# First rows' root mostly on VectorE, keys split ahead of the weights, and GpSimd scaling the output projection's pieces itself

## The chip, the cores and the metric

The kernel runs on one core of one Trainium2 chip. The metric is device time in microseconds (us) for one execution. The kernel before took 2051.89 us (median of three runs, 2051.29 to 2052.78).

## The reference

Sixteen sequences of 256 rows with 512 columns go through one layer. First a layer norm, then cross attention with 16 heads of 128 on a context of the same size, added to the input; then a second layer norm and a gated feed-forward part with block-quantised operands, added again. The first half is what the change touches:

```python
x = x + _L0_xattn_ref(_layernorm(x), ctx, Wq, Wk, Wv, Wo)
    q = (inputs_q @ Wq).reshape(b, sq, H, HD) * (1.0 / np.sqrt(HD))
    k = (inputs_kv @ Wk).reshape(b, skv, H, HD)
    v = (inputs_kv @ Wv).reshape(b, skv, H, HD)
    attn = softmax(einsum('bqhd,bkhd->bhqk', q, k))
    return einsum('bhqk,bkhd->bqhd', attn, v).reshape(b, sq, H * HD) @ Wo
x = x + _L0_ffn_ref(_layernorm(x), w_gate, w_up, w_down)
```

## The kernel before

All five engines run one program each, with an order written out by hand and counting semaphores between them. The attention part goes over 64 quads of four steps each; a step i = 4n + k is one head group. In a step TensorE does, in this order, the key projection K and the query projection (12 matmuls each into one bank), the context product of an earlier step, the scores, the value projection V (12), and from step 5 on the output projection (6) (`quad` in the TensorE program). To keep accuracy each float32 operand is split into two float16 parts: an upper part that ScalarE writes (`hi`, L610) and a lower part, the operand times its scale less the upper part, that VectorE writes (`lo`, L762). K of step i+1 waits for VectorE's lower part of q and k of step i.

The attention weights come in four chunks of eight pieces of 1024 columns. Pieces 0, 2, 4, 6 hold query and key weights, 1 and 5 value weights (`V_AT`), 3 and 7 output weights (`O_AT`). Each is staged in float32 and split the same way: ScalarE's upper part (L618), then VectorE's lower part for even pieces. For odd pieces ScalarE also writes the staged piece back multiplied by its scale (L621), and GpSimd subtracts (L442). Pieces 0 to 3 of chunk 0 (`EARLY` = 4) are split ahead of the first quad, the other 28 two per step, an even and an odd one, in the first 14 steps: in steps 0, 2, 4, ... the odd one is of the value weights, in steps 1, 3, 5, ... of the output weights. GpSimd waits for `piece_hi`, and TensorE waits for the lower parts by `wait_split`. SyncE's queue reloads a staging place when its piece has been subtracted.

Ahead of the first quad, VectorE takes the statistics of the first 256 rows (L977, L980), GpSimd computes the reciprocal root with a power and one Newton step in six small operations (`rstd`, L433 to L438), VectorE normalises (L777), and TensorE transposes through the identity (L1191), behind 30 warm-up matmuls on zeroed data (L1187). The split of the first keys and of xT follows.

In a step VectorE's order is: lower part of q and k, maximum (L923), lower part of the context, on some steps one operation of a later x or key row, scaling of the row sums (L940), their reciprocal (L943), lower part of v, lower part of the probabilities (L950), and last its piece of the weights. ScalarE's is: upper part of q and k, of the context, the even piece, the exponentials (L654), upper part of v, of the probabilities (L664), on some steps one of a key or x row, and the odd piece.

Of the kernel before, what the change touches and what calls it, by code (L numbers as in the profile page):

```python
# [36 lines left out]
ALU = mybir.AluOpType  # L37
# [3 lines left out]
P = 128  # L41
# [23 lines left out]
EARLY = PIECES - QUAD  # L65


QK_AT, V_AT, O_AT = (0, 2, 4, 6), (1, 5), (3, 7)
# [13 lines left out]
def build(nc, kvt, wattn, wffn, xtok, out):  # L82
# [4 lines left out]
    with ctx:  # L87
# [60 lines left out]
        def free_part(chunk, part, pc, pieces):  # L148
# [27 lines left out]


        names = """waited ident_ready zeroed first_x_loaded first_kv_loaded
            first_stats first_aggr first_step first_rstd first_xn first_tr first_hi first_kv_hi first_lo
            stage_loaded0 stage_loaded1 stage_loaded2 stage_loaded3 piece_hi piece_lo_even piece_lo_odd  # L180
            x_loaded kv_loaded stats_done aggr_done rstd_step rstd_done xn_ready x_hi x_lo xT_loaded kv_hi kv_lo
            s_done max_done exp_done sum_scaled rec_done
            qk_done qk_hi qk_lo c_done c_hi c_lo v_done v_hi v_lo p_hi p_lo pt_loaded0 pt_loaded1 o_done o_added
# [12 lines left out]
        def wait_apart(eng, name, value):  # L196

            eng.wait_ge(sm[name], value)
            eng.sem_inc(sm["waited"], 1)  # L199
# [17 lines left out]
        def piece(chunk, pc, part):  # L217
            return wall[:, bass.ds(chunk * (2 * WCHUNK) + part * WCHUNK + pc * PIECE, PIECE)]
# [5 lines left out]
        def staged(chunk, pc):  # L224

            if isinstance(chunk, int) and chunk == 0:
                return first_stage[:, pc * PIECE:(pc + 1) * PIECE]
            return stages[pc % SLOTS]
# [172 lines left out]
        def _(eng):  # L401
# [22 lines left out]
            def rstd(rows, width, aggr, step, done, m):  # L424

                def then(ins, k):
                    ins.then_inc(sm[step], 1)
                    wait_apart(eng, step, 5 * m + k)
                wait_apart(eng, aggr, m + 1)
                r = [rs[0:rows, width * a:width * (a + 1)] for a in range(6)]  # L430
                var = mv[0:rows, 1:2 * width:2]
                half_, eps = [powers[0:rows, a:a + 1].to_broadcast([rows, width]) for a in range(2)]
                then(eng.tensor_tensor(r[1], var, eps, ALU.add), 1)  # L433
                then(eng.tensor_tensor(r[2], r[1], half_, ALU.pow), 2)
                then(eng.tensor_tensor(r[3], r[2], r[2], ALU.mult), 3)
                then(eng.tensor_tensor(r[4], r[3], r[1], ALU.mult), 4)
                then(eng.tensor_scalar(r[5], r[4], -0.5, 1.5, ALU.mult, ALU.add), 5)
                eng.tensor_tensor(r[0], r[2], r[5], ALU.mult).then_inc(sm[done], 1)  # L438

            def split_piece(chunk, pc):  # L440
                wait_apart(eng, "piece_hi", chunk * PIECES + pc + 1)
                eng.tensor_tensor(piece(chunk, pc, 1), staged(chunk, pc), piece(chunk, pc, 0), ALU.subtract  # L442
                                  ).then_inc(sm["piece_lo_odd"], 1)

# [90 lines left out]

            load_x(0)
            load_kv(0)
            rstd(P, 2, "first_aggr", "first_step", "first_rstd", 0)
            slot1 = acc[:, 2 * D:4 * D].rearrange("p (t d) -> p t d", t=2)
            eng.dma_start(slot1, xtok[0].rearrange("t p d -> p t d")).then_inc(sm["acc_loaded"], 16)  # L540
            for pc in range(1, EARLY, 2):
# [65 lines left out]
        def _(eng):  # L607
# [4 lines left out]
            def split_piece(chunk, pc):  # L612
                if isinstance(chunk, int) and chunk == 0:
                    eng.wait_ge(sm["first_loaded"][pc], 16)
                else:
                    eng.wait_ge(sm[f"stage_loaded{pc % SLOTS}"],
                                16 * ((chunk - 1) * (PIECES // SLOTS) + pc // SLOTS + 1))
                last = eng.activation(piece(chunk, pc, 0), staged(chunk, pc), ACT.Copy, scale=W_SCALE)  # L618
                if pc % 2:

                    last = eng.activation(staged(chunk, pc), staged(chunk, pc), ACT.Copy, scale=W_SCALE)  # L621
                last.then_inc(sm["piece_hi"], 1)
# [66 lines left out]


            eng.preload_act_table(ACT.Exp)
            split_piece(0, 0)
            for m in range(QPB):
                hi(prep_slot(kvT, m, 0), first_kv(m), X_SCALE, "first_kv_loaded", 16, "first_kv_hi")
            split_piece(0, 1)
            for tile_ in range(2):
                hi(first_slot(xT, tile_, 0), first_bank[tile_][:, :].rearrange("p (c f) -> p c f", c=KC), X_SCALE,
                   "first_tr", tile_ + 1, "first_hi")
            for pc in range(2, EARLY):
                split_piece(0, pc)  # L700
            def even(n):
                return None if n % 2 else n // 2
# [54 lines left out]
        def _(eng):  # L757
# [214 lines left out]

            eng.wait_ge(sm["first_x_loaded"], 16)
            for tile_ in range(2):
                eng.bn_stats(stat[:, 6 * tile_:6 * tile_ + 6], half(first_x, tile_)).then_inc(sm["first_stats"], 1)  # L977
# [1 line left out]
            for tile_ in range(2):  # L979
                last = eng.bn_aggr(mv[:, 2 * tile_:2 * tile_ + 2], stat[:, 6 * tile_:6 * tile_ + 6])  # L980
            last.then_inc(sm["first_aggr"], 1)
            split_piece(0, 0)
            eng.wait_ge(sm["first_rstd"], 1)
            for tile_ in range(2):
                apply(half(first_norm, tile_), half(first_x, tile_), P, tile_).then_inc(sm["first_xn"], 1)
            for m in range(QPB):
                lo(prep_slot(kvT, m, 1), first_kv(m), prep_slot(kvT, m, 0), X_SCALE,
                   "first_kv_hi", m + 1, "first_lo")
            for tile_ in range(2):
                lo(first_slot(xT, tile_, 1), first_bank[tile_][:, :].rearrange("p (c f) -> p c f", c=KC),  # L990
                   first_slot(xT, tile_, 0), X_SCALE, "first_hi", tile_ + 1, "first_lo")
# [313 lines left out]
```

## Time and profile before

| | |
|---|---|
| median of three runs | 2051.89 us |
| profiled execution | 2051.55 us |
| its span, first to last instruction | 2050.0 us |
| TensorE busy | 2021.3 us, 99% |
| VectorE busy | 1536.7 us, 75% |
| ScalarE busy | 1000.2 us, 49% |
| GpSimd busy | 740.2 us, 36% |

In a timeline row the first number is the start in us from the start of the span, the second the time from the start of the group to the end of its last operation; in brackets stands how long the engine sat idle before it and what ended that. PE is TensorE, DVE VectorE, ACT ScalarE, POOL GpSimd, SP SyncE. Operations of one engine are pipelined, so the end of one lies up to 0.1 us (on TensorE 0.16) behind the start of the next.

### The profile page before, as it was taken

The page shows a single profiled execution, that of the slowest core. Times are in us where ns is not written, and L with a number is a line of the kernel's source. Part 1 is how long each engine was busy: PE and PEld are TensorE (multiplying, and loading weights), DVE is VectorE, ACT ScalarE, POOL GpSimd, SP SyncE. Part 2 cuts the span into 40 slices and gives each one's busy share as a digit, 9 for nine tenths or more (in the row PEclk, how much of TensorE's full clock was granted, in tenths as well). Part 3 has the DMA queues.
Part 4 walks back from the last instruction along what each step waited for, and adds up shares of the span by engine and source line. Part 5 has one row for each costly group of instructions (what it writes and reads, how often), then busy time and mean ns, then how long its engine had stood idle before and what let it go on. Part 6 is the DMA issues. An engine that isn't in the chain of part 4 may idle for free. (4 is left out here: it accounts for less than half of the span.)

```text
span 2050.0 us, 45754 instructions
## 1 busy us (share of the span) xinstructions
PE 2021.3 (99%) x15430; PEld 1506.2 (73%) x15430; DVE 1536.7 (75%) x3340; ACT 1000.2 (49%) x2682; POOL 740.2 (36%) x881
## 2 busy tenths in 40 slices
PE   8999999999999999999999999999999999999998
PEld 6888878788888888878888888888888874444443
DVE  6767777777777877777777777776665558888887
ACT  8955545455555455555454555455555453222332
POOL 5422232323333333323333333331111006777776
PEclk9999999999999999999999999999999999999999
DMA  8834444444444444444444445443333274454554
GB/s 257 211 72 84 86 91 86 91 90 86 90 91 91 91 88 87 91 91 91 91 86 87 90 89 91 91 86 72 69 70 71 55 168 80 78 92 83 88 87 85
DMA packets 455038, 193.26 MB, mean 94 GB/s; under 512 B 418400, under 2 KB 431200, under 8 KB 454848
## 3 DMA queue, kind: packets, MB, share of 16 engines
q1 hardware_dynamic: 432640, 139.52, 35.3%
q0 software_dynamic: 15872, 44.97, 9.2%
q10 hardware_dynamic: 6336, 6.29, 1.0%
q8 instruction: 112, 1.84, 0.4%
q14 instruction: 78, 0.64, 0.1%
HBM read 61.21 MB, written 27.26 MB: 43 GB/s over the span
## 5 line engine op out<-in xcount | busy, mean ns | idle before, releaser
L1097 PE MATMUL b_qk<-kvT,attn_weights 128*128 128x256 f16 x3072 | 377.2, 273 | 3.5 <-DVE qk L762 2.9
L1097 PE MATMUL b_v<-attn_weights,kvT 128*128 128x256 f16 x3072 | 377.2, 273 | 0.0
L1097 PE MATMUL b_qk<-xT,attn_weights 128*128 128x256 f16 x3072 | 377.2, 273 | 0.0
L654 ACT ACTIVATE prob<-b_s,nmax 128x256 f32<-128x256 f32 x514 | 239.2, 470 | 276.1 <-DVE nmax L923 274.2
L1097 PEld LDWEIGHTS b_qk<-kvT,attn_weights 128*128 128x128 f16 x3072 | 300.2, 98 | 92.7 <-issue 4.9
L950 DVE SCALAR_TENSOR_TENSOR psplit<-prob,rrec,psplit 128x256 f16<-128x256 f32 x514 | 306.5, 637 | 79.2 <-ACT psplit L664 79.2
L762 DVE SCALAR_TENSOR_TENSOR qk<-b_qk,qk 128x512 f16<-128x512 f32 x256 | 176.7, 690 | 246.0 <-ACT qk L610 238.4
L610 ACT ACTIVATE qk<-b_qk 128x512 f16<-128x512 f32 x256 | 152.5, 596 | 426.4 <-PE b_qk L1097 426.2
L1097 PEld LDWEIGHTS b_qk<-xT,attn_weights 128*128 128x128 f16 x3072 | 300.6, 98 | 34.8
L1097 PEld LDWEIGHTS b_v<-attn_weights,kvT 128*128 128x128 f16 x3072 | 300.6, 98 | 34.8
L664 ACT ACTIVATE psplit<-prob,rrec 128x256 f16<-128x256 f32 x514 | 233.0, 500 | 67.8 <-DVE rrec L943 67.8
L1097 PE MATMUL b_c<-probT,vbuf 128*128 128x256 f16 x1554 | 212.0, 273 | 3.1 <-DMA probT<-psplit 3.0
L1097 PE MATMUL b_s<-qk 128*128 128x256 f16 x1542 | 210.3, 273 | 0.0
L1152 PE MATMUL b_o<-attn_weights,cbuf 128*128 128x512 f16 x768 | 186.6, 379 | 0.0
L1152 PE MATMUL b_w<-attn_weights,cbuf 128*128 128x512 f16 x768 | 186.6, 379 | 0.0
L923 DVE TENSOR_REDUCE nmax<-b_s 128x2 f32<-128x512 f32 x257 | 177.1, 689 | 3.7 <-PE b_s L1097 3.3
L1097 PEld LDWEIGHTS b_c<-probT,vbuf 128*128 128x128 f16 x1554 | 151.3, 98 | 23.2 <-DMA probT<-psplit 4.5
L1097 PEld LDWEIGHTS b_s<-qk 128*128 128x128 f16 x1542 | 150.9, 98 | 17.4
L463 POOL TENSOR_TENSOR ffn_magic_rounded<-ffn_y,ffn_magic_rounded 128x512 f32<-128x512 f32 x48 | 60.7, 1265 | 230.1 <-DVE ffn_magic_rounded L823 230.1
L566 POOL TENSOR_TENSOR attn_weights<-attn_weights,inner_scale 128x1024 bf16<-128x1024 bf16 x63 | 120.2, 1908 | 49.2 <-DVE attn_weights L1028 43.1
L421 POOL DMA_DIRECT2D kvrow<-kvt x61 | 35.6, 584 | 241.9 <-DVE kvT L762 218.7
L1152 PEld LDWEIGHTS b_w<-attn_weights,cbuf 128*128 128x128 f16 x768 | 75.1, 98 | 63.8
(133 smaller groups left out, 2642.0 us busy)
## 6 DMA issues: line engine op xcount, KB each, us to landing
ffn_w<-wffn SPq DMA_DIRECT2D x48, 256.0 KB, 2.9
acc<-xtok POOLq DMA_DIRECT2D x16, 512.0 KB, 4.9
out<-acc POOLq DMA_DIRECT2D x16, 512.0 KB, 3.3
xrow<-xtok POOLq DMA_DIRECT2D x31, 256.0 KB, 3.2
kvrow<-kvt POOLq DMA_DIRECT2D x61, 128.0 KB, 2.4
out<-attn_weights POOLq DMA_DIRECT2D x30, 256.0 KB, 4.5
stage<-wattn SPq DMA_DIRECT2D x12, 512.0 KB, 4.6
ffn_scratch<-ffn_t SPq DMA_DIRECT2D x48, 128.0 KB, 2.5
```

The source lines that it names most:

```text
L421: eng.dma_start(kvrow[:, :], kvt[bass.ds((r + QPB) & (NQ - 1), 1), :, :].rearrange("g p f -> p (g f)")).then_inc(sm["kv_loaded"], 16)
L463: eng.tensor_tensor(wr, wy[:, :], wc, ALU.add).then_inc(sm["ffn_add"], 1)
L566: eng.tensor_tensor(by_block(q), by_block(q), spread(i_scale), ALU.mult).then_inc(sm["i_q"], 1)
L610: eng.activation(dst, src, ACT.Copy, scale=scale).then_inc(sm[done], 1)
L654: last = eng.activation(half(prob, q, 256), half(bS, q, 256), ACT.Exp, bias=nmax[:, q:q + 1], scale=1.0, accum_out=rsum[:, q:q + 1])
L664: eng.activation(p_part(k, q, 0), half(prob, q, 256), ACT.Copy, scale=rrec[:, q:q + 1]).then_inc(sm["p_hi"], 1)
L762: eng.scalar_tensor_tensor(out=dst, in0=src, scalar=scale, in1=hi_part, op0=ALU.mult, op1=ALU.subtract).then_inc(sm[done], 1)
L923: eng.tensor_reduce(nmax[:, :], bS[:, :].rearrange("p (q f) -> p q f", q=2), AX_X, ALU.max, negate=True).then_inc(sm["max_done"], 1)
L950: last = eng.scalar_tensor_tensor(out=p_part(k, z, 1), in0=half(prob, z, 256), scalar=rrec[:, z:z + 1], in1=p_part(k, z, 0), op0=ALU.mult, ...
L1097: last = eng.matmul(out, l, r, start=(a == 0), stop=(a == len(pairs) - 1))
L1152: last = eng.matmul(o_bank[tile_][:, :], l, r, start=(u % 8 == 0 and at == 0), stop=(u % 8 == 7 and at == len(pairs) - 1))
```

## The change

Three things. The reciprocal root of the first rows: the sum with epsilon and the Newton step go to VectorE (`first_rstd`), and GpSimd keeps the power alone. The order ahead of the first quad: ScalarE splits the first keys ahead of piece 0, and piece 1 after the two xT operations; VectorE subtracts piece 0 after the keys. The odd pieces of the output weights (3 and 7): ScalarE writes only the upper part, and GpSimd multiplies the staged piece by the scale, waits for itself (`piece_scaled`) and then subtracts.

```diff
@@ -439,6 +439,11 @@
 
             def split_piece(chunk, pc):
                 wait_apart(eng, "piece_hi", chunk * PIECES + pc + 1)
+                if pc in O_AT:
+                    at = chunk * len(O_AT) + O_AT.index(pc) + 1
+                    eng.tensor_scalar(staged(chunk, pc), staged(chunk, pc), W_SCALE, None, ALU.mult
+                                      ).then_inc(sm["piece_scaled"], 1)
+                    wait_apart(eng, "piece_scaled", at)
                 eng.tensor_tensor(piece(chunk, pc, 1), staged(chunk, pc), piece(chunk, pc, 0), ALU.subtract
                                   ).then_inc(sm["piece_lo_odd"], 1)
 
@@ -535,7 +540,9 @@
 
             load_x(0)
             load_kv(0)
-            rstd(P, 2, "first_aggr", "first_step", "first_rstd", 0)
+            wait_apart(eng, "first_step", 1)
+            eng.tensor_tensor(rs[:, 4:6], rs[:, 2:4], powers[:, 0:1].to_broadcast([P, 2]), ALU.pow
+                              ).then_inc(sm["first_pow"], 1)
             slot1 = acc[:, 2 * D:4 * D].rearrange("p (t d) -> p t d", t=2)
             eng.dma_start(slot1, xtok[0].rearrange("t p d -> p t d")).then_inc(sm["acc_loaded"], 16)
             for pc in range(1, EARLY, 2):
@@ -616,7 +623,7 @@
                     eng.wait_ge(sm[f"stage_loaded{pc % SLOTS}"],
                                 16 * ((chunk - 1) * (PIECES // SLOTS) + pc // SLOTS + 1))
                 last = eng.activation(piece(chunk, pc, 0), staged(chunk, pc), ACT.Copy, scale=W_SCALE)
-                if pc % 2:
+                if pc in V_AT:
 
                     last = eng.activation(staged(chunk, pc), staged(chunk, pc), ACT.Copy, scale=W_SCALE)
                 last.then_inc(sm["piece_hi"], 1)
@@ -689,14 +696,13 @@
 
 
             eng.preload_act_table(ACT.Exp)
-            split_piece(0, 0)
             for m in range(QPB):
                 hi(prep_slot(kvT, m, 0), first_kv(m), X_SCALE, "first_kv_loaded", 16, "first_kv_hi")
-            split_piece(0, 1)
+            split_piece(0, 0)
             for tile_ in range(2):
                 hi(first_slot(xT, tile_, 0), first_bank[tile_][:, :].rearrange("p (c f) -> p c f", c=KC), X_SCALE,
                    "first_tr", tile_ + 1, "first_hi")
-            for pc in range(2, EARLY):
+            for pc in range(1, EARLY):
                 split_piece(0, pc)
             def even(n):
                 return None if n % 2 else n // 2
@@ -972,6 +978,22 @@
 
 
 
+            def first_rstd():
+
+                def then(ins, k):
+                    ins.then_inc(sm["first_step"], 1)
+                    eng.wait_ge(sm["first_step"], k)
+                eng.wait_ge(sm["first_aggr"], 1)
+                r = [rs[:, 2 * a:2 * a + 2] for a in range(6)]
+                eps = powers[:, 1:2].to_broadcast([P, 2])
+                eng.tensor_tensor(r[1], mv[:, 1:4:2], eps, ALU.add).then_inc(sm["first_step"], 1)
+                eng.wait_ge(sm["first_pow"], 1)
+                then(eng.tensor_tensor(r[3], r[2], r[2], ALU.mult), 2)
+                then(eng.tensor_tensor(r[4], r[3], r[1], ALU.mult), 3)
+                then(eng.tensor_scalar(r[5], r[4], -0.5, 1.5, ALU.mult, ALU.add), 4)
+                eng.tensor_tensor(r[0], r[2], r[5], ALU.mult).then_inc(sm["first_rstd"], 1)
+                eng.wait_ge(sm["first_rstd"], 1)
+
             eng.wait_ge(sm["first_x_loaded"], 16)
             for tile_ in range(2):
                 eng.bn_stats(stat[:, 6 * tile_:6 * tile_ + 6], half(first_x, tile_)).then_inc(sm["first_stats"], 1)
@@ -979,13 +1001,13 @@
             for tile_ in range(2):
                 last = eng.bn_aggr(mv[:, 2 * tile_:2 * tile_ + 2], stat[:, 6 * tile_:6 * tile_ + 6])
             last.then_inc(sm["first_aggr"], 1)
-            split_piece(0, 0)
-            eng.wait_ge(sm["first_rstd"], 1)
+            first_rstd()
             for tile_ in range(2):
                 apply(half(first_norm, tile_), half(first_x, tile_), P, tile_).then_inc(sm["first_xn"], 1)
             for m in range(QPB):
                 lo(prep_slot(kvT, m, 1), first_kv(m), prep_slot(kvT, m, 0), X_SCALE,
                    "first_kv_hi", m + 1, "first_lo")
+            split_piece(0, 0)
             for tile_ in range(2):
                 lo(first_slot(xT, tile_, 1), first_bank[tile_][:, :].rearrange("p (c f) -> p c f", c=KC),
                    first_slot(xT, tile_, 0), X_SCALE, "first_hi", tile_ + 1, "first_lo")
```

ScalarE's program ahead of the first quad, before. `attn_weights<-attn_weights` is a weight piece, `kvT<-attn_weights` a row group of the first keys, `xT<-` the transposed first rows; the last row is the first operation of step 0.

```order
L618 ACTIVATE attn_weights<-attn_weights 128x1024
L610 ACTIVATE kvT<-attn_weights 128x4x64 x4
L618 ACTIVATE attn_weights<-attn_weights 128x1024
L621 ACTIVATE attn_weights<-attn_weights 128x1024
L610 ACTIVATE xT<-b_x 128x4x128
L610 ACTIVATE xT<-b_w 128x4x128
L618 ACTIVATE attn_weights<-attn_weights 128x1024 x2
L621 ACTIVATE attn_weights<-attn_weights 128x1024
L610 ACTIVATE qk<-b_qk 128x512
```

And after:

```order
L617 ACTIVATE kvT<-attn_weights 128x4x64 x4
L625 ACTIVATE attn_weights<-attn_weights 128x1024
L617 ACTIVATE xT<-b_x 128x4x128
L617 ACTIVATE xT<-b_w 128x4x128
L625 ACTIVATE attn_weights<-attn_weights 128x1024
L628 ACTIVATE attn_weights<-attn_weights 128x1024
L625 ACTIVATE attn_weights<-attn_weights 128x1024 x2
L617 ACTIVATE qk<-b_qk 128x512
```

Piece 1, two operations that stood ahead of the two xT rows, stands behind them, and the scaled copy of piece 3 is gone.

GpSimd's program from the first root to the root of the next rows (`128x1`), before:

```order
L433 TENSOR_TENSOR rs<-mv,minus_half_and_eps 128x2
L434 TENSOR_TENSOR rs<-rs,minus_half_and_eps 128x2
L435 TENSOR_TENSOR rs<-rs 128x2
L436 TENSOR_TENSOR rs<-rs 128x2
L437 TENSOR_SCALAR rs<-rs 128x2
L438 TENSOR_TENSOR rs<-rs 128x2
L540 DMA acc<-xtok 128x2x512
L442 TENSOR_TENSOR attn_weights<-attn_weights 128x1024 x2
L433 TENSOR_TENSOR rs<-mv,minus_half_and_eps 128x1
```

And after:

```order
L544 TENSOR_TENSOR rs<-rs,minus_half_and_eps 128x2
L547 DMA acc<-xtok 128x2x512
L447 TENSOR_TENSOR attn_weights<-attn_weights 128x1024
L444 TENSOR_SCALAR attn_weights<-attn_weights 128x1024
L447 TENSOR_TENSOR attn_weights<-attn_weights 128x1024
L433 TENSOR_TENSOR rs<-mv,minus_half_and_eps 128x1
```

One power is left of the six operations, and ahead of the subtraction of piece 3 there is a multiply (L444).

## Rows read from the trace of the kernel before

**Rows 1.** The page, busy time of each engine.
```profile
PE 2021.3 (99%) x15430; PEld 1506.2 (73%) x15430; DVE 1536.7 (75%) x3340; ACT 1000.2 (49%) x2682; POOL 740.2 (36%) x881
```

**Rows 2.** Waits of TensorE, 44 to 1680 us: engine, line waited for: us in total, times, longest.
```profile
PE b_c L1097 <- DMA probT<-psplit: 3.0, 3, 1.1
```

**Rows 3.** Timeline of TensorE at the start: start us, us, operation, [idle before <-releaser].
```profile
5.00 6.36 PE L1187 MATMUL b_s<-vbuf 128*128 128x256 f16 x30 [5.00 <-POOL vbuf L413]
...
11.19 0.60 PE L1191 MATMUL b_x<-ident,attn_weights 128*128 128x128 f32 x4
...
12.82 1.47 PE L1097 MATMUL b_qk<-kvT,attn_weights 128*128 128x256 f16 x12 [0.60 <-DVE kvT L762]
...
18.06 1.47 PE L1097 MATMUL b_qk<-kvT,attn_weights 128*128 128x256 f16 x12
...
23.64 1.47 PE L1097 MATMUL b_qk<-kvT,attn_weights 128*128 128x256 f16 x12 [0.18 <-DVE qk L762]
...
42.57 1.47 PE L1097 MATMUL b_qk<-kvT,attn_weights 128*128 128x256 f16 x12 [1.27 <-DVE qk L762]
...
49.10 1.47 PE L1097 MATMUL b_qk<-kvT,attn_weights 128*128 128x256 f16 x12
```

**Rows 4.** Timeline of ScalarE at the start.
```profile
12.32 0.59 ACT L610 ACTIVATE xT<-b_w 128x512 f16<-128x512 f32 x1
...
15.64 0.60 ACT L610 ACTIVATE qk<-b_qk 128x512 f16<-128x512 f32 x1
...
22.20 0.57 ACT L610 ACTIVATE qk<-b_qk 128x512 f16<-128x512 f32 x1
...
27.35 1.04 ACT L621 ACTIVATE attn_weights<-attn_weights 128x1024 f32<-128x1024 f32 x1
...
28.30 0.58 ACT L610 ACTIVATE qk<-b_qk 128x512 f16<-128x512 f32 x1
...
34.45 0.57 ACT L610 ACTIVATE qk<-b_qk 128x512 f16<-128x512 f32 x1
...
41.13 0.57 ACT L610 ACTIVATE qk<-b_qk 128x512 f16<-128x512 f32 x1
...
47.59 0.57 ACT L610 ACTIVATE qk<-b_qk 128x512 f16<-128x512 f32 x1
```

**Rows 5.** Timeline of VectorE at the start.
```profile
11.26 1.42 DVE L762 SCALAR_TENSOR_TENSOR kvT<-attn_weights,kvT 128x256 f16<-128x256 f32 x4
...
13.89 1.86 DVE L762 SCALAR_TENSOR_TENSOR attn_weights<-attn_weights 128x1024 f16<-128x1024 f32 x1
...
18.82 0.14 DVE L940 TENSOR_SCALAR rsum<-rsum 128x2 f32<-128x2 f32 x1
...
25.18 0.17 DVE L940 TENSOR_SCALAR rsum<-rsum 128x2 f32<-128x2 f32 x1 [0.26 <-ACT prob L654]
...
26.93 1.22 DVE L762 SCALAR_TENSOR_TENSOR attn_weights<-attn_weights 128x1024 f16<-128x1024 f32 x1
...
43.27 0.80 DVE L762 SCALAR_TENSOR_TENSOR xsplit<-xnorm,xsplit 128x512 f16<-128x512 f32 x1
```

**Rows 6.** The weights' tile, 0 to 45 us: duration ns min/median/max, first and last start.
```profile
L762 DVE SCALAR_TENSOR_TENSOR attn_weights<-attn_weights x4: 1218/1222/1859, 8.6 to 26.9; 128x1024 f16<-128x1024 f32 x4
```

**Rows 7.** Timeline of GpSimd at the start.
```profile
11.92 2.75 POOL L442 TENSOR_TENSOR attn_weights<-attn_weights 128x1024 f16<-128x1024 f32 x1 [0.43 <-ACT attn_weights L621]
...
15.93 2.13 POOL L442 TENSOR_TENSOR attn_weights<-attn_weights 128x1024 f16<-128x1024 f32 x1 [1.26 <-ACT attn_weights L621]
```

**Rows 8.** Timeline of VectorE, 271 to 273 us.
```profile
271.82 0.65 DVE L940 TENSOR_SCALAR rsum<-rsum 128x2 f32<-128x2 f32 x1 [0.76 <-ACT prob L654]
```

**Rows 9.** Timeline of GpSimd, 271 to 273 us.
```profile
271.40 1.05 POOL L470 TENSOR_TENSOR ffn_b<-ffn_magic_rounded,ffn_scale 128x512 bf16<-128x512 f32 x1 [3.65 <-DMA ffn_t<-ffn_b]
```

**Rows 10.** GpSimd's clip of 512 columns (L467): duration ns min/median/max.
```profile
L467 POOL TENSOR_SCALAR ffn_magic_rounded<-ffn_magic_rounded x48: 606/614/892, 136.4 to 1369.0; 128x512 f32<-128x512 f32 x48
```

**Rows 11.** DMA issues: count, KB each, median us to landing.
```profile
ffn_magic_rounded<-wattn SPq DMA_DIRECT2D x6, 512.0 KB, 4.9
```

More of the change, by code:

```diff
@@ L178, in build @@
         names = """waited ident_ready zeroed first_x_loaded first_kv_loaded
-            first_stats first_aggr first_step first_rstd first_xn first_tr first_hi first_kv_hi first_lo
-            stage_loaded0 stage_loaded1 stage_loaded2 stage_loaded3 piece_hi piece_lo_even piece_lo_odd
+            first_stats first_aggr first_step first_pow first_rstd first_xn first_tr first_hi first_kv_hi first_lo
+            stage_loaded0 stage_loaded1 stage_loaded2 stage_loaded3 piece_hi piece_scaled piece_lo_even piece_lo_odd
             x_loaded kv_loaded stats_done aggr_done rstd_step rstd_done xn_ready x_hi x_lo xT_loaded kv_hi kv_lo
```

## The prediction

> **What bounds the kernel now.** I read four views, in this order. The page first: TensorE is busy for 99% of the span [rows 1], so a change that leaves its work alone can give back only what TensorE waits. Then the waits of TensorE in the attention part from 44 us on: three waits of about 1 us each for a transposing DMA, and nothing else in 1636 us [rows 2]. So from 44 us to the feed-forward part TensorE sets the pace, and whatever the change does to the other engines there is hidden unless it comes late by more than their slack. The feed-forward part at the end has none of the changed lines. Then the timeline of TensorE at the start, and there the room is. The reader is to look at the starts of the key projections K(i), i counting the steps of one head, four to a quad. One step is 18.06 - 12.82 = 5.24 us of matmuls. From K(1) to K(5) it takes 42.57 - 18.06 = 24.51 us for 4 x 5.24 = 20.96, so 3.55 us are stalls. From step 5 on the output projection joins, a step is 49.10 - 42.57 = 6.53 us, and there are no stalls [rows 3]. Last the timelines of ScalarE, VectorE and GpSimd there. I call A(i) the start of ScalarE's first operation of step i, the upper half of q and k. VectorE's lower half follows it, and K(i+1) starts 1.44 us after A(i): 23.64 after 22.20, 42.57 after 41.13 [rows 3, 4]. A(i) follows A(i-1) by 6.56, 6.10, 6.15, 6.68 and 6.46 us [rows 4]. That is ScalarE's own work, most of it on weight pieces, and it is more than 5.24. So up to K(5) ScalarE is the bound, and from there TensorE is by a hair: A(5) + 1.44 = 49.03, K(6) at 49.10.
>
> The sum is made against the profiled execution, 2051.55 us (span 2050.0 and 1.55 around it), which lies 0.34 under the median of the three runs, 2051.89.
>
> **The root of the first rows.** Six small GpSimd operations become one there and five on VectorE. On paper the root is ready some 1.9 us sooner. But the transposes that need it stand in TensorE's queue behind 30 warm-up matmuls, which start at 5.00, end at 11.36 by the profile and have the first transpose close behind them, at 11.19 [rows 3]. Neither the warm-up nor the clearing of its operand changes. So the transposes don't move, nor does ScalarE's second upper half of xT at 12.32 [rows 4]. Gain: nothing. If this cover were gone it would be up to 1.9 us at the very start.
>
> **Piece order on ScalarE.** The keys' upper halves go ahead of piece 0, which costs nothing, since ScalarE then waits for the transposes anyway. But piece 1 and its scaled copy, two operations that filled that wait, now stand behind the xT operations. Before, three operations of a piece lay between 12.32 + 0.48 = 12.80 and A(0) = 15.64, 0.95 us each [rows 4]. Now there are four (piece 1 twice, piece 2, piece 3): A(0) = 12.80 + 4 x 0.95 = 16.60, 0.95 later.
>
> **Who holds whom.** Three rows of before show that VectorE and GpSimd hold each other. VectorE's subtraction of piece 2 took 1.86 us where its kind takes 1.22; GpSimd's subtraction had 0.78 to go when it started (11.92 + 2.75 = 14.67 against 13.89), so the hold was 0.64 [rows 5 to 7]. GpSimd's took 2.75 instead of 2.13 while VectorE's four key operations ran to 12.68, 0.76 into it [rows 5, 7]. And the tiny scaling of the row sums took 0.65 us instead of 0.17 when GpSimd had 0.63 to go [rows 5, 8, 9]. Each hold is what the other has to go, less 0.15. I use that rule.
>
> In the Trainium skill, GPSIMD Engine Reference, section Key points, the shared SBUF interfaces are said to collide with VectorE instructions that have two SBUF inputs or run in a 2-port mode. Only the second half could cover the row-sum scaling, which has one input of two elements; were it not covered, rival B below would be the case. The trace's 0.65 us speaks for a hold, in one instance.
>
> **The first step.** Piece 1's scaled copy on ScalarE is 13.75 to 14.79; GpSimd's subtraction starts 0.19 after such an end (15.74 to 15.93 [rows 4, 7]), so 14.98 to 17.11. VectorE's subtraction of piece 2 is issued at 15.78 and held 1.18, to 18.18. Behind it queue the lower half of q and k, which could start at 17.2 and starts at 18.1, 0.87 late, then the maximum and the row sums. GpSimd's new multiply of piece 3 is ready when its subtraction ends, but VectorE's waiting operation goes first: held until about 18.0, then 1.03, its subtraction 19.3 to 21.4. The multiply is not in the trace. Nearest is a GpSimd tensor_scalar on 512 columns at 0.61 us [rows 10]; with 0.19 of it fixed, 1024 columns are 1.03. The other end is 2.13, the two-input operation on the same size [rows 7]. I take 1.03, since it is the same kind. The row sums are scaled 3.18 us after A(0) (18.82 after 15.64 [rows 4, 5]), here 0.87 more: 20.65, inside GpSimd's subtraction, with 0.75 to go: held 0.60. So A(1) = 22.20 + 0.95 + 0.87 + 0.60 = 24.62.
>
> **The output projection's pieces.** ScalarE loses one operation, 0.95 us (28.30 - 27.35), for each of pieces 3 and 7 of four chunks [rows 4]. GpSimd gains a multiply, a wait for it and 0.19 us. Let A' be the A that is earlier by 0.95. The multiply is issued at A' + 0.29, held by VectorE's subtraction of the even piece until A' + 0.80 (26.93 + 1.22 = 28.15 against 27.35 [rows 4, 5]), less 0.15, and ends at A' + 1.68. The subtraction then lies at A' + 1.88 to A' + 4.01.  The next row sums are scaled at A' + 2.98 (25.18 - 22.20), with 1.03 to go: held 0.88. The reciprocal, ScalarE's upper half of the probabilities, its pieces and the next A queue behind. So an edit that takes off 0.95 gives back 0.88. In an odd quad (steps 4 to 7) the first step has VectorE's lower half of x at A + 2.14 ahead of the row sums (43.27 - 41.13), and there ScalarE's x operation lets the multiply run unheld: subtraction A' + 1.51 to A' + 3.64, lower half held 1.35, row sums 1.11 late.
>
> The sum, step by step:
> - A(2) = 24.62 + 6.10 - 0.95 = 29.77 (before 28.30)
> - A(3) = 29.77 + 6.15 + 0.88 = 36.80 (34.45)
> - A(4) = 36.80 + 6.68 - 0.95 = 42.53 (41.13)
> - A(5) = 42.53 + 6.46 + 1.11 = 50.10 (47.59)
> - K(6) = 50.10 + 1.44 = 51.54 against 49.10: 2.4 us later.
>
> After that TensorE's 6.53 a step outruns ScalarE's: A(6), after 5.2 in a step without the scaled copy, is 55.3, so K(7) would be 56.7 by it and is 58.07 by TensorE; the lag is no longer added to and never recovered. The pieces come in time: piece 3 of chunk 1 is subtracted at 42.53 + 3.64 = 46.2, its projection is due at 42.53 + 1.44 + 5.24 = 49.2. The next load into its staging place, 4.9 us [rows 11], is there by 51.5, and ScalarE wants it after 54. The forecast is 2051.55 + 2.44 = 2054.0, on the median's footing 2054.3. That is the predicted time, and the rivals below are on the median's footing too.
>
> **Rivals.** B: the row sums are not held, only operations with two large inputs. For it: one instance of the hold in the trace; against it: its size fits the rule. Then 0.60 and 0.88 go and nothing else: A(5) is 48.62, K(6) 50.06, 1.0 later, 2052.9.
>
> C: no new holds at all, GpSimd's longer work slips between VectorE's. A(1) is then 23.15, A(2) 28.30, A(3) 34.45, A(4) 40.18, K(5) 41.62, and K(6) is TensorE's at 48.15: 0.95 sooner, 2050.9. Against it: three holds in the rows.
>
> D: the full gain that the stalls allow, 3.55 plus some 0.3 at K(0), if the transposes did come early: 2048.0. Against it is the warm-up [rows 3].
>
> E: the multiply costs 2.13. Each subtraction moves 1.1 back. The first row sums are held 1.8 instead of 0.6, those of step 2 up to 2.0 instead of 0.88, those of step 4 0.8 more: 3.1 more in all, 2057.4. It decides slower from a multiply of about 1.6 us on, where half of this is reached. Against it: the 0.61 us at 512 columns.
>
> **How the numbers follow.** Forecast A 0.60, B 0.15, C 0.08, D 0.03, E 0.12, and 0.02 for other losses. About 0.2% (4.1 us) is what a measurement of this kernel can tell from no change: below 2047.8 is faster, above 2056.0 slower. A has its own range of 2053.2 to 2056.2, and a little of it lies above, so slower has 0.12 + 0.02 + 0.02 = 0.16. D reaches the limit only just, faster has 0.03. Same has 0.81. The range takes in C and half of E: 2050.8 to 2057.0.
>
> **What would show it.** TensorE's transposes stay at 11.2; A(0) at 16.6; the value projection of step 0 waits for piece 1 and starts near 17.2; VectorE's subtraction of piece 2 lasts 2.4 us; GpSimd's multiplies last about 1.03 alone; row-sum scalings of 0.8 to 1.0 us after pieces 3 and 7; K(6) at 51.5, and 6.53 a step from there. Wrong if the multiply lasts over 1.6 us, if the row sums stay at 0.17 us with GpSimd busy, or if K(6) is at or under 49.1.

## The result

The changed kernel takes 2054.64 us (median of 22 runs, 2052.72 to 2056.54). The kernel before took 2051.61 us beside it on the same chip (22 runs, 2048.89 to 2053.67). The ratio is 1.0015, with a 95% interval of 1.0009 to 1.0021: 3.0 us more. The interval does not hold 1, so the loss is real, but it is smaller than the 0.2% (4.1 us) within which the prediction counts a time as no change. The profiled execution took 2055.55 us, with a span of 2053.5.

### The profile after

The busy line of the page, answering to [rows 1], and TensorE's waits from 44 to 1680 us, answering to [rows 2]:

```profile
PE 2024.2 (99%) x15430; PEld 1510.7 (74%) x15430; DVE 1555.9 (76%) x3345; ACT 999.3 (49%) x2674; POOL 762.6 (37%) x884
```

```profile
PE b_c L1119 <- DMA probT<-psplit: 3.2, 2, 2.2
```

TensorE is busy for 2.9 us more, though its work is the same: a hint that it ran slowly somewhere. GpSimd has 22 us more, although five small operations left it: at least 2.8 for each of the eight multiplies. And one of the waits on the transposing DMA is 2.2 us.

The timeline of TensorE at the start, answering to [rows 3] (start, duration, engine, line, operation, and in brackets the idle time before it and what ended it):

```profile
4.99 4.77 PE L1209 MATMUL b_s<-vbuf 128*128 128x256 f16 x30 [4.99 <-POOL vbuf L413]
9.60 0.60 PE L1213 MATMUL b_x<-ident,attn_weights 128*128 128x128 f32 x4
...
12.14 1.48 PE L1119 MATMUL b_qk<-kvT,attn_weights 128*128 128x256 f16 x12 [1.51 <-DVE attn_weights L768]
...
24.12 1.47 PE L1119 MATMUL b_qk<-kvT,attn_weights 128*128 128x256 f16 x12 [1.32 <-DVE qk L768]
...
49.57 1.47 PE L1119 MATMUL b_qk<-kvT,attn_weights 128*128 128x256 f16 x12
...
54.55 0.83 PE L1119 MATMUL b_c<-probT,vbuf 128*128 128x256 f16 x6 [2.20 <-DMA probT<-psplit]
...
56.18 2.77 PE L1119 MATMUL b_v<-attn_weights,kvT 128*128 128x256 f16 x12
...
60.14 1.47 PE L1119 MATMUL b_qk<-kvT,attn_weights 128*128 128x256 f16 x12
```

The transposes start at 9.60, not 11.19, and the first key projection at 12.14, 0.68 sooner than before. K(6) starts at 49.57, only 0.47 later than before. Then, inside step 6, the context product waits 2.20 us for the transposed probabilities, and the matmuls behind it run slowly. K(7) starts at 60.14. Before it was at 55.64, 6.54 behind 49.10. So K(7) is 4.5 us late, and 4.0 of it came in that one step.

The same timeline of GpSimd, answering to [rows 7]:

```profile
13.40 2.12 POOL L447 TENSOR_TENSOR attn_weights<-attn_weights 128x1024 f16<-128x1024 f32 x1 [4.99 <-ACT attn_weights L628]
15.50 3.74 POOL L444 TENSOR_SCALAR attn_weights<-attn_weights 128x1024 f32<-128x1024 f32 x1
19.43 2.13 POOL L447 TENSOR_TENSOR attn_weights<-attn_weights 128x1024 f16<-128x1024 f32 x1 [0.18 <-POOL attn_weights L444]
...
29.28 3.15 POOL L444 TENSOR_SCALAR attn_weights<-attn_weights 128x1024 f32<-128x1024 f32 x1 [2.65 <-ACT attn_weights L625]
...
41.88 2.77 POOL L444 TENSOR_SCALAR ffn_magic_rounded<-ffn_magic_rounded 128x1024 f32<-128x1024 f32 x1 [3.34 <-ACT attn_weights L625]
44.84 2.13 POOL L447 TENSOR_TENSOR attn_weights<-ffn_magic_rounded,attn_weights 128x1024 f16<-128x1024 f32 x1 [0.18 <-POOL ffn_magic_rounded L444]
46.91 0.79 POOL L538 DMA_DIRECT2D acc<-xtok  x1
47.70 0.56 POOL L417 DMA_DIRECT2D xrow<-xtok  x1
```

The multiply (L444) lasts 2.77 us undisturbed, where the forecast had 1.03. The subtraction of piece 3 of chunk 1 ends at 46.97, and GpSimd issues its two loads behind it. In the kernel before it ended at 43.53:

```profile
41.40 2.13 POOL L442 TENSOR_TENSOR attn_weights<-ffn_magic_rounded,attn_weights 128x1024 f16<-128x1024 f32 x1 [4.54 <-ACT ffn_magic_rounded L621]
```

The end of the subtraction also frees SyncE's reload of the staging place. In SyncE's queue (SPq, the start of the issue), after and then before:

```profile
47.00 0.33 SPq L266 DMA_DIRECT2D ffn_magic_rounded<-wattn  x1
47.81 1.24 SPq L284 DMA_TRANSPOSE probT<-psplit  x1
```

```profile
43.55 0.33 SPq L266 DMA_DIRECT2D ffn_magic_rounded<-wattn  x1
46.16 1.24 SPq L284 DMA_TRANSPOSE probT<-psplit  x1
```

Before, the reload had 2.6 us of lead on the transposing DMA of step 4, and GpSimd's loads stood at 43.5 and 44.2. Now 1.25 MB of loads are issued between 46.91 and 47.70, and the transposing DMA right behind them. The DMA view from 44 to 60 us has (KB each where given, median us from issue to landing), after and then before:

```profile
probT<-psplit SPq DMA_TRANSPOSE x2, 6.8
```

```profile
probT<-psplit SPq DMA_TRANSPOSE x3, 4.0
```

These are medians of the few transposing DMAs in that stretch. The one of step 4, taken alone, landed 6.7 us after its issue in the changed kernel, at 54.51, and 4.0 us after it before. The context product starts at 54.55, so the 2.20 us are this late landing.

The landing is late for two reasons. The DMA was issued 1.65 us later (47.81 against 46.16), since GpSimd held VectorE's lower half of the probabilities just ahead of it (2.06 us instead of 0.88; the rest is the 0.47 of K(6)), and it took 2.7 us longer. Before, it landed at 50.12, 1.6 us ahead of its reader at 51.73, and in the changed kernel the reader was due at 52.35. Worked out from these numbers, the late issue alone would have made no wait (47.81 + 4.0 = 51.8), and the slow transfer alone about 0.5 us (46.16 + 6.7 = 52.9).

The view by stretches (columns: busy us of TensorE, its weight loads, VectorE, ScalarE, GpSimd, then the granted clock) shows the slow matmuls behind the wait: the clock was granted at 0.50, the lower of its two levels, 1.2 GHz.

```profile
54.00:56.00 2.00, 1.45 (x12) 1.23 (x13) 0.70 (x2) 0.38 (x1) 2.00 (x1) 0.89 0.98 365
56.00:58.00 2.00, 2.00 (x11) 1.45 (x10) 1.02 (x2) 0.71 (x1) 1.81 (x2) 0.50 1.52 179
58.00:60.00 2.00, 2.00 (x11) 1.11 (x10) 0.67 (x3) 1.78 (x7) 1.62 (x2) 0.76 1.11 145
```

From the context product to the projection is 54.55 to 60.14, 5.59 us, for what takes 3.91 before (51.73 to 55.64): 1.7 us for the clock. In the kernel before:

```profile
51.73 0.82 PE L1097 MATMUL b_c<-probT,vbuf 128*128 128x256 f16 x6
```

VectorE, answering to [rows 5, 8]:

```profile
8.61 1.00 DVE L783 TENSOR_SCALAR attn_weights<-attn_weights,mv,rs 128x512 f32<-128x512 f32 x2
...
14.19 2.41 DVE L768 SCALAR_TENSOR_TENSOR attn_weights<-attn_weights 128x1024 f16<-128x1024 f32 x1 [0.90 <-ACT attn_weights L625]
...
18.98 0.29 DVE L946 TENSOR_SCALAR rsum<-rsum 128x2 f32<-128x2 f32 x1
...
20.05 2.18 DVE L956 SCALAR_TENSOR_TENSOR psplit<-prob,rrec,psplit 128x256 f16<-128x256 f32 x2 [0.26 <-ACT psplit L671]
...
24.82 2.10 DVE L768 SCALAR_TENSOR_TENSOR kvT<-kvrow,kvT 128x256 f16<-128x256 f32 x1
...
33.29 2.13 DVE L956 SCALAR_TENSOR_TENSOR psplit<-prob,rrec,psplit 128x256 f16<-128x256 f32 x2 [0.32 <-ACT psplit L671]
...
45.59 2.06 DVE L956 SCALAR_TENSOR_TENSOR psplit<-prob,rrec,psplit 128x256 f16<-128x256 f32 x2 [0.31 <-ACT psplit L671]
```

The normalisation starts at 8.61 instead of 10.34. GpSimd's subtractions hold VectorE, but not where forecast: the row sums take 0.29 us, and the two operations on the probabilities behind them take 2.1 to 2.2 instead of 0.88, because the longer multiply moved the subtraction past the row sums. In step 1 the subtraction of a value piece holds the lower half of a key row, 2.10 us instead of 0.58. ScalarE, answering to [rows 4], starts its steps at 14.99, 22.52, 28.99, 35.46, 41.59 and 48.06.

At the end of the attention part the last key projection starts at 1682.00 us, 1.7 later than before (1680.27), not 4.5. In the rest of that part the kernel before has three waits of about 1 us on this DMA [rows 2] and the changed one has one. From there to the end of the span, mostly the feed-forward part, whose lines the change does not touch, it took 371.5 us against 369.7. In this profile the clock stood at 0.50 in two stretches there (1759 to 1762 and 1892 to 1895 us), in that of the kernel before at 1.00 in the same work. A second profile of the changed kernel (`e9_changed_again`, below) has neither stretch and took 369.1, so this difference can't be put down to the change. The slow stretches also add to TensorE's busy time. A single pair of profiles is therefore no measure of 3 us. The medians are.

### The profile page after: what moved, and what is told of

Same layout as the page of the kernel before. It is cut to its first block and busy times, and to the rows that moved or that the text cites. A ratio compares the mean times of both kernels' runs of the same rounds, so it can differ in the third digit from the quotient of the medians.

```text
span 2053.5 us, 45757 instructions
## 1 busy us (share of the span) xinstructions
PE 2024.2 (99%) x15430; PEld 1510.7 (74%) x15430; DVE 1555.9 (76%) x3345; ACT 999.3 (49%) x2674; POOL 762.6 (37%) x884
## 5 line engine op out<-in xcount | busy, mean ns | idle before, releaser
L956 DVE SCALAR_TENSOR_TENSOR psplit<-prob,rrec,psplit 128x256 f16<-128x256 f32 x514 | 316.4, 656 | 80.2 <-ACT psplit L671 80.2
```

The lines of the kernel that those rows point to most:

```text
L956: last = eng.scalar_tensor_tensor(out=p_part(k, z, 1), in0=half(prob, z, 256), scalar=rrec[:, z:z + 1], in1=p_part(k, z, 0), op0=ALU.mult, ...
```

## The experiments

The theory after the result: the time is lost by the long multiply, through the late loads and the transposing DMA. The rivals: the new order ahead of the first quad costs it; or held VectorE operations do, as forecast. The first four kernels tell these apart, e5, e6 and e8 test the mends, and e7, e9 and e10 show how the first microseconds vary. Where a ratio is given, the kernel ran 11 times and the kernel before 27 times; e3, e7, e9 and e10 have one profiled run each.

**Each half alone.** `e1_scale_only` is the kernel before with GpSimd's scaling, `e2_root_and_order` the changed kernel with ScalarE's scaling. The edit of the second, against the changed kernel:

```diff
-                if pc in O_AT:
-                    at = chunk * len(O_AT) + O_AT.index(pc) + 1
-                    eng.tensor_scalar(staged(chunk, pc), staged(chunk, pc), W_SCALE, None, ALU.mult
-                                      ).then_inc(sm["piece_scaled"], 1)
-                    wait_apart(eng, "piece_scaled", at)
...
-                if pc in V_AT:
+                if pc % 2:
```

> The kernel before with the GpSimd scaling of the output weights' pieces alone; root and order are as before. Theory M (the loss comes from GpSimd's multiply, 2.77 us where 1.03 was reckoned, which ends its subtraction late and so delays loads and transposes): all of the loss is here, K(7) 3 to 5 us behind before's 55.64, the time 2 to 4 us above before (ratio 1.001 to 1.002). Theory O (the loss comes from piece 1's place behind the xT operations on ScalarE, the scaling only passes it on): K(6) at 48.2 to 49.5, no wait of over 1 us before step 7, the time within 0.5 us of before.

> The changed kernel with the scaling of the output weights' pieces given back to ScalarE; root and order stay changed. Theory M: the loss is gone, K(0) some 0.7 us earlier than before if the warm-up ends early and A(0) within 0.5 us of it, K(6) between 48.5 and 50.0, the time within 1 us of before (0.9995 to 1.0005). Theory O: K(6) at 50 or later and the time 1 to 3 us above before.

Measured: 2055.35 us with the scaling alone, ratio 1.0017 (1.0008 to 1.0026), and 2052.21 with root and order alone, 1.0003 (0.9994 to 1.0012). The second is 1.1 us above the kernel before, unresolved, where under 1 was expected. The scaling carries the loss. TensorE's timeline with the scaling alone:

```profile
11.15 0.66 PE L1196 MATMUL b_x<-ident,attn_weights 128*128 128x128 f32 x4 [1.16 <-DVE attn_weights L782]
...
49.90 1.47 PE L1102 MATMUL b_qk<-kvT,attn_weights 128*128 128x256 f16 x12
...
54.56 0.83 PE L1102 MATMUL b_c<-probT,vbuf 128*128 128x256 f16 x6 [1.88 <-DMA probT<-psplit]
...
58.48 1.47 PE L1102 MATMUL b_qk<-kvT,attn_weights 128*128 128x256 f16 x12
```

The same wait in the same place, without the half clock behind it: K(7) is 2.8 late, a little under the 3 to 5 expected. The kernel with root and order alone has no wait there (K(6) 49.34, K(7) 55.87).

**What the multiply costs by its form.** `e3_forms` computes the eight multiplies in four forms:

```diff
+                    if form in (0, 4):
+                        eng.tensor_scalar(st, st, W_SCALE, None, ALU.mult).then_inc(sm["piece_scaled"], 1)
+                    if form in (1, 5):
+                        eng.tensor_scalar(st, st, W_SCALE, 1.0, ALU.mult, ALU.mult).then_inc(sm["piece_scaled"], 1)
+                    if form in (2, 6):
+                        eng.tensor_scalar(half(st, 0), half(st, 0), W_SCALE, None, ALU.mult)
...
+                    if form in (3, 7):
+                        eng.tensor_tensor(st, st, powers[:, 2:3].to_broadcast([P, PIECE]), ALU.mult
```

> The changed kernel with the multiply in four forms on the eight pieces, in order: pieces 1 and 5 one operation with one immediate on 1024 columns as in the change, 2 and 6 the same with a second multiply by 1.0, 3 and 7 two operations of 512 columns, 4 and 8 a tensor_tensor with a broadcast constant. If it is the form with one immediate that is slow: 2.77 us for forms one and three (2 x 1.4) and about 1.1 to 1.2 for form two, as the clip of 512 columns with two immediates at 0.61 says. If it is the size: two times 0.6 for form three, 2.7 for one and two. If it is writing back in place: all forms 2.1 or more. The tensor_tensor is expected at 2.1 to 2.7 us, as the subtraction's 2.13.

GpSimd's timeline:

```profile
30.85 1.42 POOL L449 TENSOR_SCALAR attn_weights<-attn_weights 128x1024 f32<-128x1024 f32 x1 [2.64 <-ACT attn_weights L636]
...
43.62 1.50 POOL L451 TENSOR_SCALAR ffn_magic_rounded<-ffn_magic_rounded 128x512 f32<-128x512 f32 x1 [3.62 <-ACT attn_weights L636]
45.10 1.48 POOL L452 TENSOR_SCALAR ffn_magic_rounded<-ffn_magic_rounded 128x512 f32<-128x512 f32 x1
...
55.49 2.27 POOL L455 TENSOR_TENSOR ffn_magic_rounded<-ffn_magic_rounded,minus_half_and_eps 128x1024 f32<-128x1024 f32 x1 [2.78 <-ACT attn_weights L636]
```

With two immediates (L449) 1.42 us, partly held; with one, 1.48 us for each 512 columns; as a two-input operation 2.27. The same element count, type and engine: only the form of the instruction differs. The row that the forecast scaled from [rows 10] is a clip, which has two immediates. This kernel was the slowest, 2060.38 us. Its TensorE shows the same wait and the same slow matmuls:

```profile
57.77 0.83 PE L1130 MATMUL b_c<-probT,vbuf 128*128 128x256 f16 x6 [3.53 <-DMA probT<-psplit]
...
59.42 2.77 PE L1130 MATMUL b_v<-attn_weights,kvT 128*128 128x256 f16 x12
```

**The collision taken apart.** `e4_acc_early` issues the 512 KB load of `acc` ahead of the late subtraction:

```diff
+                        if isinstance(r, int) and r == 0 and k == QUAD - 1:
+                            eng.dma_start(acc[:, 0:2 * D].rearrange("p (t d) -> p t d", t=2),
+                                          xtok[1:2].rearrange("b t p d -> p (b t) d")).then_inc(sm["acc_loaded"], 16)
...
-                    if more and (q == 0 if first_s else q == 3):
+                    if more and (False if first_s else q == 3):
```

> The changed kernel with the load of the second sequence's rows (512 KB) issued by GpSimd ahead of the split of piece 3 of chunk 1 instead of behind it, near 42 us instead of 46.9. If the wait of 2.20 us at step 6 (54.55) is the transpose standing behind two 512 KB and one 256 KB loads that are issued within 0.9 us ahead of it: the transpose of step 4 lands 1 to 2 us sooner, the wait falls to 0 to 1.2 us, the matmuls behind it stay at full clock (273 ns), K(7) at 56 to 58 instead of 60.14, the time 1.5 to 3.5 us under the changed kernel. If the loads are not the cause (only VectorE's late lower half of the probabilities is): wait and K(7) unchanged within 0.5 us.

Measured: 2053.26 us, 1.0010 (1.0001 to 1.0020). The load, now issued at 38.81, is 9 us away from the transposing DMA at 48.31, and step 6 has no wait (K(6) 51.11, K(7) 57.64, 6.53 apart). But there is one in step 5:

```profile
47.18 0.83 PE L1122 MATMUL b_c<-probT,vbuf 128*128 128x256 f16 x6 [0.86 <-DMA probT<-psplit]
```

Its transposing DMA, issued at 41.40 behind the load that was moved, took 5.7 us; the one of the same step in the changed kernel took 3.6. So the edit moved part of the collision one step forward.

At the old place the transposing DMA took 5.2 us, between 6.7 in the changed kernel and 4.0 before (6.4 with the scaling alone, 4.0 with the short form below). One load fewer beside it takes 1.5 us off the landing, so the loads issued together make part of it. That step 6 has no wait comes as much from TensorE, which reaches K(6) 1.5 us later than in the changed kernel. The gain in time is not resolved: 1.4 us below the changed kernel's median where 1.5 to 3.5 were expected, with overlapping intervals. With no wait in step 6, and one of 0.86 us in step 5, this kernel still lies above the kernel before, by the edge of its interval. So the wait of step 6 is not shown to be the whole loss.

**The short form.** `e5_two_immediates` is the changed kernel with a second, idle factor:

```diff
-                    eng.tensor_scalar(staged(chunk, pc), staged(chunk, pc), W_SCALE, None, ALU.mult
+                    eng.tensor_scalar(staged(chunk, pc), staged(chunk, pc), W_SCALE, 1.0, ALU.mult, ALU.mult
```

> The changed kernel with the multiply given a second multiply by 1.0, the form that took 1.42 us instead of 2.77. Theory M (the multiply's length ends the subtraction late, and loads and transposes collide behind it): row sums are now held 0.8 to 1.0 us after pieces 3 and 7, so K(6) comes later than the changed kernel's 49.57, at 50 to 51; but the subtraction of piece 3 of chunk 1 ends by 46 instead of 46.97 and the wait at step 6 falls under 0.5 us: K(7) at 56.5 to 57.6 instead of 60.14, the time 1 to 3.5 us under the changed kernel. Theory O (ScalarE's order sets the loss): nothing of over 0.5 us changes in the time.

Measured: 2051.77 us, 0.9999 (0.9990 to 1.0008). The loss is gone, and this interval and the changed kernel's (1.0009 to 1.0021) do not overlap. GpSimd, VectorE and TensorE:

```profile
42.85 1.04 POOL L444 TENSOR_SCALAR ffn_magic_rounded<-ffn_magic_rounded 128x1024 f32<-128x1024 f32 x1 [3.62 <-ACT attn_weights L625]
```

```profile
20.49 0.87 DVE L946 TENSOR_SCALAR rsum<-rsum 128x2 f32<-128x2 f32 x1
...
32.87 0.95 DVE L946 TENSOR_SCALAR rsum<-rsum 128x2 f32<-128x2 f32 x1 [0.76 <-ACT prob L661]
```

```profile
51.64 1.47 PE L1119 MATMUL b_qk<-kvT,attn_weights 128*128 128x256 f16 x12
...
58.17 1.47 PE L1119 MATMUL b_qk<-kvT,attn_weights 128*128 128x256 f16 x12
```

This is the kernel that the prediction worked out. The multiply is 1.04 us, the row sums are held as its rule says, and ScalarE's steps start at 16.51, 24.62, 29.78, 36.83, 42.56 and 50.19, forecast 16.60, 24.62, 29.77, 36.80, 42.53 and 50.10. K(6) is at 51.64, forecast 51.54. K(6) and K(7) are 0.6 us later than expected before this run. No wait stands in step 6: the same 1.25 MB of loads are issued from 46.15 to 46.91, but the transposing DMA 1.9 us behind the last of them, at 48.76, and it lands after 4.0 us. In the changed kernel it was issued 0.1 us behind the last, and took 6.7. So the row sums are held here and the loss is gone: the holds of the forecast are not what makes it. And the time is not 2.4 us above the kernel before: the profiled execution is above it (2055.19), the median of eleven is not. In the profile the warm-up ended late, at 11.28, and the later waits on the transposing DMA come to 3.7 us; both vary from one execution to the next.

**The order of piece 1.** `e6_piece1_ahead` has root and keys first, ScalarE's scaling, and piece 1 ahead of the two xT operations; `e8_piece1_and_two` has both mends:

```diff
             split_piece(0, 0)
+            split_piece(0, 1)
             for tile_ in range(2):
...
-            for pc in range(1, EARLY):
+            for pc in range(2, EARLY):
```

> Root on VectorE and keys first, ScalarE scaling all odd pieces, and piece 1 split ahead of the two xT operations again. If piece 1's place is what ScalarE loses at the start: A(0) at 14.8 to 15.3 when the warm-up ends near 9.6 to 10 (against 15.97 with piece 1 behind), K(6) at 48.2 to 48.8 instead of 49.34, and the time 0.3 to 1 us under before. If it is not: A(0) within 0.2 of 15.97.

> The changed kernel with both mends: the two-immediate multiply and piece 1 ahead of the xT operations. If both theories hold a part: A(0) 14.3 to 15.0 (bounded by the query projection's end), K(6) between 49 and 50, no wait of over 0.5 us at step 6, the time within 1 us of before and 2 to 4 us under the changed kernel.

Measured: 2050.95 us, 0.9996 (0.9987 to 1.0005), and 2050.68, 0.9995 (0.9986 to 1.0004). Both intervals hold 1, so neither is shown to beat the kernel before. With a late warm-up, A(0) is 15.61 in e6 where piece 1 is ahead, and 16.37 to 16.56 in the three kernels where it is behind: 0.76 to 0.95 us for the order. In e8 K(6) is at 48.68 and K(7) at 55.21, with no wait between.

**The first microseconds.** `e7_root_only` is the kernel before with VectorE's root, `e9_changed_again` and `e10_before_again` are the two kernels once more.

> The kernel before with the first rows' root on VectorE alone, order and scaling as before. If the warm-up covers the root, the transposes start where it ends, at 9.6 to 11.2 by the clock's rise, and with an early rise K(0) comes at 12.2 to 12.5 instead of the 13.04 of an early rise with the old root; with a late rise (11.2) K(0) stays at 12.8 and nothing is won.

> The changed kernel once more, for a second profile. If the wait at step 6 belongs to the kernel and not to one execution: a wait of 1.5 to 3.5 us for the transposed probabilities near 52 to 58 us again, K(7) 2 us or more beyond K(6) + 6.53. K(0) at 12.0 to 12.2 whether the warm-up ends at 9.6 or 11.2 (VectorE's piece 0 is the bound), A(0) at 15.0 with an early end and 16.6 with a late one. If the wait was chance: under 1 us.

> The kernel before once more. If the root was its bound at the start whenever the warm-up ends early: transposes at 11.0 to 11.2 with an idle TensorE ahead of them, K(0) 12.8 to 13.1, K(6) 49.0 to 49.4, and no wait at step 6. If the root never was the bound: transposes at the end of the warm-up, at 9.6 to 10.6 with an early one.

Measured: 2051.29, 2052.87 and 2050.10 us. TensorE in the changed kernel again, and then in the kernel before again:

```profile
10.98 0.60 PE L1213 MATMUL b_x<-ident,attn_weights 128*128 128x128 f32 x4
...
16.96 1.48 PE L1119 MATMUL b_v<-attn_weights,kvT 128*128 128x256 f16 x12 [0.58 <-POOL attn_weights L447]
...
50.93 1.47 PE L1119 MATMUL b_qk<-kvT,attn_weights 128*128 128x256 f16 x12
...
55.63 0.83 PE L1119 MATMUL b_c<-probT,vbuf 128*128 128x256 f16 x6 [1.92 <-DMA probT<-psplit]
...
59.55 1.47 PE L1119 MATMUL b_qk<-kvT,attn_weights 128*128 128x256 f16 x12
```

```profile
10.81 0.65 PE L1191 MATMUL b_x<-ident,attn_weights 128*128 128x128 f32 x4 [0.40 <-DVE attn_weights L777]
```

The same code has its transposes at 9.60 in one execution and at 10.98 in another. The 30 warm-up matmuls take 4.77 to 6.36 us over all twelve profiles, by when the clock rises: TensorE runs 6 or 7 of them in a microsecond and then 12. The first clock record of a trace, at the full level, begins at 7.75 us in the profile of the changed kernel and at 11.02 in that of the kernel before, and in all twelve a later one goes with a longer warm-up. Where the view by stretches gives 1.00 ahead of that, the trace has no record. Where the warm-up matmuls end late, the root is covered, as forecast. Where they end early, the old root is the bound: the transposes wait 0.40 us here and 1.16 in e1. e7 has them at 10.60 and K(0) at 12.48, against 12.70 in e10 with a warm-up as long as its own. With root and order changed, K(0) is at 12.00 to 12.34. So the new root gains 0.2 us in e7 and, with the order, up to 1.0 against e1's 13.04, in some executions, and these few tenths lie below what the times can show.

## Why the prediction came out as it did

The forecast was 2054.3 us with 0.81 on no change, and the median is 2054.64. The size was right partly by luck: one step failed, and what it caused came to much the same sum by another way. One of the prediction's own signs of being wrong, a multiply of over 1.6 us, was met, and several of its marks were missed: transposes at 9.60, not 11.2, A(0) at 14.99, not 16.6, K(6) at 49.57, not 51.5.

- **The failed step: the multiply at 1.03 us.** It lasts 2.77 us undisturbed and up to 3.74 held. It lies outside even the bound of 2.13, which took the two-input operation for the dearest form. The 1.03 was scaled from a row of another form of tensor_scalar; for that form it is right (1.04 in e5). Rival E had a long multiply too (2.13), and worked out from it longer holds of the row sums, 2057.4. That is not what happened.
- **The row sums.** Forecast: held 0.60, 0.88 and 1.11. In the changed kernel they are held 0.1 to 0.2, since the subtraction comes later and meets the probabilities instead (1.2 to 1.3 held, with some slack on VectorE before its next bound work). With the short multiply the row sums of steps 0 and 2 are held 0.70 and 0.78, and in step 4 the lower half of x is held 1.36 (forecast 0.60, 0.88 and 1.35): the rule (what the other has to go, less 0.15) stood, the place moved with the size of the multiply. In the first of these GpSimd had 0.85 to go, and the hold was 0.70. Rival B, no holds of row sums, is out by e5.
- **A term that the sum did not have: the transposing DMA.** The forecast looked at whether the reload comes in time for its reader (it does), not at what it is issued next to. All four profiles with a long multiply and the loads unmoved (the changed kernel twice, e1, e3) have a wait of 1.9 to 3.5 us in step 6; no other profile has one. K(6) is 0.5 late and K(7) 4.5 in the first profile, 1.8 and 3.9 in the second. The forecast had 2.4 for both. Up to K(7) this wait is the larger part of the lag. Of the median's 3.0 us that is not shown: at the last key projection 1.7 and 1.8 us of the lag are left against the first profile of the kernel before (3.2 and 3.3 against its second), and e4 gains no resolved time without the wait.
- **The root gains nothing.** Half right: covered when the warm-up runs to 11.3, 0.2 us by itself at K(0) when it ends sooner (e7 against e10), of which nothing is left at K(6) (48.98 against 48.97). The forecast took the one profile for the rule.
- **Piece 1 behind xT costs 0.95 at A(0).** Right where its condition held: 16.37 to 16.56 against 15.61. With an early warm-up everything there starts sooner and A(0) is 14.99.
- **VectorE's piece 2 lasts 2.4.** Right, 2.41. The value projection of step 0 waits for piece 1 only with the late warm-up (16.96, 0.58 of waiting).
- **A lag at K(6) is kept to the end.** Right for TensorE's own work, 6.53 a step. But waits on the transposing DMA come and go later on, 0.7 to 3.8 us in all per profile (step 6 left out), and the rest of the span, with the feed-forward part, varies by up to 2.4 us (369.1 to 371.5, both in the changed kernel). A chain that is right to 0.1 us at 50 us (e5) did therefore not give the median to 2 us.

Not settled: why the form with one immediate is slow; how the long multiply's 3.0 us divide between the wait of step 6, the clock behind it and the rest, since the half clock is in two profiles (waits of 2.20 and 3.53 us) and absent in two (1.88 and 1.92), which fits a longer wait as its condition but is only four cases; and why e5, whose profile shows the forecast lag, is not slower in the median. The late landing goes with how closely the loads are issued ahead: the four profiles with the DMA 0.1 us behind them have 6.4 to 8.0 us, the seven with it 1.85 us or more behind the same loads 4.0 to 4.3. Why is open, and moving the transposing DMA itself ahead of the reload was not tried.

## What to carry to other kernels

Take the price of an operation from a row of its very form, the number of scalar operands included, or keep a bound that covers other forms. When an operation grows on an engine that also issues or frees loads, list what will then be issued in the same microsecond as the transfer on the critical path. And look at two profiles of the same code before calling something covered by a warm-up.

## What was not expected of the hardware

- GpSimd's tensor_scalar on float32 with one immediate took 2.77 us for 128x1024 and 1.48 for 128x512; with two immediates 1.04 for 128x1024; tensor_tensor with a broadcast column 2.27.
- The transposing DMA of step 4 landed 6.4 to 8.0 us after its issue when issued 0.1 us behind the last of 1.25 MB of loads, and 4.0 to 4.3 us after it when issued 1.85 us or more behind the same loads.
- The same 30 warm-up matmuls took 4.77 to 6.36 us from one execution to the next. From 8 to 10 us TensorE ran 11 of them in the profile of before and 21 matmuls in that of the changed kernel, where the first clock record, at full level, begins at 11.02 and at 7.75.
- A wait of 2.20 or 3.53 us of TensorE was followed by a granted clock of 0.50, one of 1.88 or 1.92 us was not.
